# Experts over 512 tokens at once, their sum transposed in one bank and turned back, the combine weight applied last, and a new order of work

## The chip, the cores and the metric

The kernel runs on one core of a Trainium2 chip. The metric is the device time of one execution in microseconds (us). The engines of a core are named as in the profile: PE (TensorE matmul) and PEld (its weight load), DVE (VectorE), ACT (ScalarE), POOL (GpSimd) and SP (SyncE, whose queue issues most DMAs here). They run side by side, each takes its own instructions in program order, and semaphores tie them together.

## The reference

One transformer layer on x of shape (2, 1024, 128), all in float32: a causal attention with 16 heads of 8 dimensions, then a mixture of experts.

```python
x = x + attention(layernorm(x))          # 16 heads, q and k normed, rope, causal
xf = layernorm(x).reshape(-1, 128)       # 2048 tokens
scores = softmax(xf @ gate_w.T)          # 16 experts in 4 groups; the 2 best groups, then the 2 best experts
combine = (one_hot(idx, 16) * weights[..., None]).sum(1)      # (token, expert), two entries not zero
h1 = einsum('td,edi->tei', xf, We1) + be1                     # every expert on every token, i = 64
h3 = einsum('td,edi->tei', xf, We3) + be3
yo = einsum('tei,eid->ted', silu(h1) * h3, We2) + be2
y = einsum('te,ted->td', combine, yo)
z = silu(xf @ ws1 + bs1) * (xf @ ws3 + bs3) @ ws2 + bs2       # shared expert
x = x + (y + z)
```

## The kernel before

The 2048 tokens are four chunks x = 0 to 3 of 512 tokens (four tiles of 128). Each chunk is prepared (norm, q/k/v, rope), goes through attention in four head groups (a = 4x to 4x+3), and then through an epilogue (onT, proj, norm2, x2T, gate, routing, cT) and the experts. In attention, `max` matmuls feed row maxima to DVE (L1157), `scores` matmuls (L783) feed exponentials on ACT (L911), and `pv` matmuls (L801) sum in bank 7; `leave` (L978, o_raw) copies that bank out at the end of a group. So the last row on L978 is the end of attention.

PSUM has eight banks of 512 float32 columns. Bank 7 holds attention's sum, bank 6 the experts' sum y, and the others are shared out.

The 16 experts are eight pairs, so that a pair's inner width is 128; with the shared expert there are UNITS = 9 units. Before the change a unit is worked on for half a chunk (HALF = 256 tokens), which makes 18 steps for each chunk and 72 in all. A step goes like this:

- PE: two matmuls of 256 columns, w1 and w3 against x2T, both into one bank (L838, L839). The trace shows a float32 matmul as two records.
- ACT: mu = (u + b1)/2 (L948), mv = v + b3 (L950), both out of that bank, which is then free; mh = tanh(mu) (L958).
- POOL (chunk 3: DVE): mv = mv * combine weight (L601). The weights have come from DRAM, spread over the partitions (comb_b, four DMAs of 512 KB for a chunk, L681), where the routing's result was stored (L673).
- DVE: mh = (mh + 1) * mu (L1246).
- POOL: mh = mh * mv (L1076).
- PE: two matmuls of 128 columns with mh as the weights and w2 as what moves, added into y, tokens on the partitions (L850). At one step of a chunk the bias be2 is added with four small matmuls (L855).

At the end of a chunk DVE adds bank 6 to xs (L1309, `final`) and SP stores it. mu, mv and mh have MOE_RING = 4 places.

The router's result goes: gate matmuls (L819), gate_read (L1207, L1208), route1 to route3 on DVE (L1218 to L1241, some 35 small operations), cT on PE (L827), combT on ACT (L1010), store and load by DMA, then the first weighting.

The order of work on each engine is the output of `plan()`: a list scheduler over named stages, each with an assumed length (LENGTHS), an urgency out of tables of numbers (PREP_WINDOWS, MOE_WINDOWS and so on) and the stages that it follows. The five engines' programs are that one list, filtered.

## Time and profile before

| | |
|---|---|
| three runs | 459.22, 461.11 (median), 461.4 us |
| the profiled execution | 462.71 us, of which the span on the core is 461.0 us |
| PE busy | 387.2 us (84%) |
| DVE busy | 352.2 us (76%) |
| ACT busy | 273.4 us (59%) |
| POOL busy | 186.8 us (41%) |

The span runs from the first to the last instruction; the remaining 1.7 us lie around it. Busy shares are means over stages in which different engines are the limit, so the stretches below matter more than these. PEclk is the share of full speed that was granted to TensorE; it has two levels, 1.2 and 2.4 GHz, which the rows show as 0.5 and 1.0 or a mix.

### The profile page before, as it was taken

The numbers are of one execution on the slowest core, as the hardware profiler recorded it, in microseconds if no ns is written. First come the engines' busy times: TensorE is split into PE (matmuls) and PEld (weight loads), VectorE is DVE, ScalarE is ACT, GpSimd is POOL, SyncE is SP. The second block draws the span as 40 slices with busy tenths as digits, with TensorE's granted clock in tenths as the row PEclk, the third lists the DMA queues.
The fourth block names the chain that finished last, engine by engine and source line by source line (L and its number), as shares of the span: only waits on it lengthen the run. The fifth ranks groups of instructions, "written<-read, shape, count | busy, mean of one in ns | idle before, by whom it ended". The sixth has DMA issues, their size and how long they took to land.

```text
span 461.0 us, 7965 instructions
## 1 busy us (share of the span) xinstructions
PE 387.2 (84%) x2663; PEld 194.1 (42%) x2663; DVE 352.2 (76%) x757; ACT 273.4 (59%) x483; POOL 186.8 (41%) x277
## 2 busy tenths in 40 slices
PE   3642867679797999999999798889999999986995
PEld 2321322213323443664334334544333273775884
DVE  4778989889878788794387799987875883678396
ACT  2523044621786584757955664439688789864784
POOL 1303926732065225464523130546202244575564
PEclk9765698575889699999999699999999999999998
DMA  5955022000050007000005005300000000800530
GB/s 144 193 101 137 2 60 79 3 1 0 1 138 1 3 19 169 1 1 1 4 23 139 2 1 126 63 1 1 2 2 0 1 3 4 197 11 1 143 67 23
DMA packets 30265, 21.54 MB, mean 47 GB/s; under 512 B 8945, under 2 KB 30098, under 8 KB 30162
## 3 DMA queue, kind: packets, MB, share of 16 engines
q1 hardware_dynamic: 28834, 19.99, 18.6%
q10 hardware_dynamic: 1392, 1.05, 0.9%
q8 instruction: 22, 0.36, 0.4%
q14 instruction: 17, 0.14, 0.1%
HBM read 13.43 MB, written 1.18 MB: 32 GB/s over the span
## 4 chain that ended last, share of the span: by engine, by line
PE 55%; DVE 25%; ACT 8%; issue 7%; POOL 2%; SPq 1%; DMA 1%; POOLq 0%; ACTq 0%; DVEq 0%
PE psum L801 13%; PE psum L783 7%; PE psum L759 7%; PE psum L850 6%; DVE mx_diag L1157 6%; PE psum L838 6%; PE psum L839 5%; DVE mx_full L1157 3%; PE psum L753 3%; PE psum L724 3%; ACT probs L911 2%; DVE nr L1095 2%; DVE mv L601 2%; DVE nr L1096 2%; PE psum L733 1%
## 5 line engine op out<-in xcount | busy, mean ns | idle before, releaser
L911 ACT ACTIVATE probs<-psum 128x1024 f32<-128x1024 f32 x144 | 141.6, 1027 | 58.7 <-PE psum L783 55.4
L1157 DVE TENSOR_REDUCE mx_diag<-psum 128x4 f32<-128x512 f32 (+2 forms) x96 | 96.6, 1039 | 26.4 <-PE psum L759 25.8
L1065 POOL TENSOR_SCALAR_AFFINE_SELECT probs<-probs 128x256 f32<-128x256 f32 (+1 forms) x112 | 47.7, 442 | 108.3 <-ACT probs L911 107.8
L1157 DVE TENSOR_REDUCE mx_full<-psum 128x2 f32<-128x1024 f32 x64 | 75.8, 1218 | 17.0 <-PE psum L759 16.7
L1076 POOL TENSOR_TENSOR mh<-mh,mv 128x256 f32<-128x256 f32 x72 | 55.5, 777 | 77.9 <-DVE mh L1246 69.5
L801 PE MATMUL psum<-probs,v_ones 128*9 128x512 f32 (+3 forms) x768 | 82.1, 519 | 1.5 <-POOL probs L1065 0.8
L783 PE MATMUL psum<-q_st,k_st 64*128 64x512 bf16 (+3 forms) x384 | 59.8, 363 | 9.7 <-ACT probs L911 6.7
L759 PE MATMUL psum<-k_st,q_st 62*128 62x512 bf16 (+3 forms) x384 | 62.7, 357 | 4.4 <-DVE mx_full L1157 2.3
L1246 DVE SCALAR_TENSOR_TENSOR mh<-mh,mu 128x256 f32<-128x256 f32 x72 | 36.5, 523 | 27.0 <-ACT mh L958 26.7
L948 ACT ACTIVATE mu<-psum,b1h 128x256 f32<-128x256 f32 x72 | 33.8, 470 | 37.0 <-PE psum L839 25.0
L850 PE MATMUL psum<-w,mh 128*128 128x128 f32 x288 | 48.1, 295 | 5.6 <-POOL mh L1076 5.5
L838 PE MATMUL psum<-x2T,w 128*128 128x256 f32 x144 | 47.7, 414 | 1.6 <-ACT mv L950 1.6
L601 POOL TENSOR_TENSOR mv<-mv,comb_b 128x256 f32<-128x256 f32 x48 | 35.4, 740 | 27.7 <-ACT mv L950 23.9
L850 PEld LDWEIGHTS psum<-w,mh 128*128 128x128 f32 x288 | 39.3, 194 | 17.3 <-POOL mh L1076 9.5
L839 PE MATMUL psum<-x2T,w 128*128 128x256 f32 x144 | 43.8, 387 | 0.0
L783 PEld LDWEIGHTS psum<-q_st,k_st 64*128 64x128 bf16 x384 | 17.5, 97 | 59.9 <-ACT probs L911 38.8
L753 PE MATMUL psum<-causal_bf,ident_bf 128*128 128x128 bf16 (+1 forms) x192 | 33.1, 259 | 10.3 <-DVE mx_diag L1157 7.1
L950 ACT ACTIVATE mv<-psum,b 128x256 f32<-128x256 f32 x72 | 33.8, 469 | 0.0
L958 ACT ACTIVATE mh<-mu 128x256 f32<-128x256 f32 x72 | 29.7, 418 | 6.8 <-PE psum L855 2.8
L759 PEld LDWEIGHTS psum<-k_st,q_st 62*128 62x128 bf16 x384 | 16.4, 95 | 35.1 <-issue 16.1
L839 PEld LDWEIGHTS psum<-x2T,w 128*128 128x128 f32 x144 | 28.2, 196 | 4.2
L753 PEld LDWEIGHTS psum<-causal_bf,ident_bf 128*128 128x128 bf16 x192 | 13.4, 101 | 39.1 <-DVE mx_diag L1157 18.6
(142 smaller groups left out, 422.4 us busy)
## 6 DMA issues: line engine op xcount, KB each, us to landing
comb_b<-combine_scratch SPq DMA_DIRECT2D x16, 512.0 KB, 8.7
q_st<-parts SPq DMA_DIRECT2D x24, 128.0 KB, 2.5
k_st<-parts SPq DMA_DIRECT2D x18, 128.0 KB, 2.4
w<-in_We SPq DMA_DIRECT2D x3, 512.0 KB
k_st<-in_c_pad SPq DMA_DIRECT2D x2, 512.0 KB, 8.0
out<-xs SPq DMA_DIRECT2D x4, 256.0 KB, 4.5
xs<-in_x SPq DMA_DIRECT2D x3, 256.0 KB, 10.3
k_st<-parts ACTq DMA_DIRECT2D x6, 128.0 KB, 3.5
```

Source lines behind the costliest of these rows:

```text
L601: engine.tensor_tensor(mv[:, at % MOE_RING, :], mv[:, at % MOE_RING, :], comb_b[:, half, u, :], ALU.mult).then_inc(weighted, 1)
L753: pe.matmul(v, ident_bf[:, :], causal_bf[:, :].unsqueeze(1).broadcast_to([P, nm, P]), start=True, stop=False, skip_group_check=True)
L759: last = pe.matmul(w[:, par, i * keys:(i + 1) * keys], q_st[r, x % 2, 2 * g + m, q0:q0 + P], k_st[r, b, 2 * g + m, k0:k0 + keys], start=(w ...
L783: last = pe.matmul(w[:, par, col:col + cols], k_st[rows(par), b, 2 * g + m, kt * P:(kt + 1) * P], q_st[rows(par), x % 2, 2 * g + m, q0:q0 ...
L801: last = pe.matmul(acc[32 * j:32 * j + VC, q0:q0 + cols], v_ones[:, b, kt, G * g + j, :], probs[:, n % P_RING, j % 2, col:col + cols], sta ...
L838: pe.matmul(w[:, 0:HALF], w1[:, u, :], rhs, start=True, stop=True)
L839: pe.matmul(w[:, HALF:CH], w3[:, u, :], rhs, start=True, stop=True).then_inc(work_full, 1)
L850: last = pe.matmul(y[:, tok * P:(tok + 1) * P], mh[:, at % MOE_RING, t * P:(t + 1) * P], w2[:, u, :], start=(n == 0 and t == 0), stop=(n = ...
L911: act.activation(probs[:, n % P_RING, :, :], wpair("scores", (s, i)), ACT.Exp, scale=SCALE).then_inc(exp_done, 1)
L1065: last = pool.affine_select(out=v, in_=v, compare_op=ALU.is_ge, fill=0.0, base=0, pattern=[[0, v.shape[1]], [1, P]], channel_multiplier=-1)
L1076: pool.tensor_tensor(mh[:, at % MOE_RING, :], mh[:, at % MOE_RING, :], mv[:, at % MOE_RING, :], ALU.mult).then_inc(h_ready, 1)
L1157: dve.tensor_reduce(dst[:, qt, :, pairs[0]:pairs[0] + nm], w, AX.X, ALU.max).then_inc(max_free, 1)
```

## The change

A unit is now worked on for the whole chunk of 512 tokens, 9 steps for a chunk and 36 in all.

- PE: v = w3 against x2T, 512 columns, into a bank of its own (`moeV`), and u = w1 against x2T into another (`moeU`).
- ACT: mv = (v + b3)/2 out of the first (`moe_v`), which frees it; mh = tanh((u + b1)/2) straight out of the second (`moe_t`), and, after a wait for that, mh = mh + 1. mu is gone.
- DVE: mv = (u + b1) * mv, with u still in PSUM (`moe_a`). This frees the second bank.
- POOL: mh = mh * mv (`moe_g`), and then the combine weight, mh = mh * comb_b (`moe_h`; in chunk 3 on DVE, `moe_h_dve`). The weight comes last, so everything ahead of it can run without it. mh has nine places now (T_RING), mv four (V_RING).
- PE: one matmul of 512 columns with w2 as the weights and mh as what moves, so y is transposed in bank 6 (features on the partitions). The bias is one matmul of 512 columns.
- At a chunk's end ACT copies bank 6 to yT (`y_leave`), PE turns it back in four transposes (`yturn`), and DVE adds it to xs.
- The weights come in two DMAs of 1 MB for a chunk (before: four of 512 KB).
- The shared unit is the first of a chunk (n = 0) and takes no weight.
- The assumed lengths and all urgency tables have new numbers, so the order is new everywhere, in attention too. rden has two places.

```diff
-P_RING, MOE_RING = 6, 4
+P_RING, V_RING, T_RING = 6, 4, 9
...
 def unit(n):
 
-    return (n, PAIRS) if n < 2 else divmod(n - 2, PAIRS)
-
+    return (n - 1) % UNITS
...
-MOE_WINDOWS = ((57.8, 72.7), (115.5, 150.2), (242.3, 392.7), (261.5, 603.0))
...
+MOE_WINDOWS = ((119.1, 212.3), (178.6, 259.5), (211.2, 383.4), (419.9, 419.9))
...
-            add("moe", (x, n), key, ("x2T_read", x), back("moe", 1))
-            pair = unit(n)[1] < PAIRS
-            add("moe_u", (x, n), key, ("halved", 0), ("moe", (x, n)), back("moe_h", MOE_RING), back("moe_u", 1))
-            add("moe_t", (x, n), key, ("moe_u", (x, n)), back("moe_y", MOE_RING), back("moe_t", 1))
...
+            add("moeV", (x, n), key, ("x2T_read", x), back("moeU", 1))
+            add("moe_v", (x, n), key, ("halved", 0), ("moeV", (x, n)), back("moe_g", V_RING), back("moe_t", 1))
+            add("moeU", (x, n), key, ("moeV", (x, n)))
+            add("moe_t", (x, n), key, ("moeU", (x, n)), ("moe_v", (x, n)), back("moe_y", T_RING))
+            add("moe_a", (x, n), key, ("moe_t", (x, n)), back("moe_a", 1))
+            add("moe_g", (x, n), key, ("moe_a", (x, n)), back("moe_g", 1))
...
-            engine.wait_ge(act_u, at + 1)
-            engine.tensor_tensor(mv[:, at % MOE_RING, :], mv[:, at % MOE_RING, :], comb_b[:, half, u, :],
-                                 ALU.mult).then_inc(weighted, 1)
+            u = unit(n)
+            if n == 1:
+                engine.wait_ge(ld_combine, 32 * (x + 1))
+            engine.wait_ge(gate_done, UNITS * x + n + 1)
+            h = mh[:, (UNITS * x + n) % T_RING, :]
+            engine.tensor_tensor(h, h, comb_b[:, u, :], ALU.mult).then_inc(weighted, 1)
...
+                        src = combine_dram[x].rearrange("(m e) q -> e m q", e=2)[e]
+                        sp.dma_start(comb_b[64 * e:64 * e + 64, :, :], src.partition_broadcast(64)
+                                     ).then_inc(ld_combine, 16)
...
-                rhs = x2T[:, x % 2, half * HALF:(half + 1) * HALF]
-                pe.matmul(w[:, 0:HALF], w1[:, u, :], rhs, start=True, stop=True)
-                pe.matmul(w[:, HALF:CH], w3[:, u, :], rhs, start=True, stop=True).then_inc(work_full, 1)
+                pe.matmul(w, (w1 if kind == "moeU" else w3)[:, unit(n), :], x2T[:, x % 2, :], start=True, stop=True
+                          ).then_inc(work_full, 1)
...
-                pe.wait_ge(h_ready, at + 1)
-                for t in range(2):
-                    tok = 2 * half + t
-                    last = pe.matmul(y[:, tok * P:(tok + 1) * P], mh[:, at % MOE_RING, t * P:(t + 1) * P], w2[:, u, :],
-                                     start=(n == 0 and t == 0), stop=(n == 2 * UNITS - 1), skip_group_check=True)
+                    pe.wait_ge(gate_done, at + 1)
+                else:
+                    pe.wait_ge(weighted, PAIRS * x + n)
+                last = pe.matmul(y, w2[:, unit(n), :], mh[:, at % T_RING, :], start=(n == 0), stop=(n == UNITS - 1),
+                                 skip_group_check=True)
                 if n == BIAS_STEP:
                     pe.wait_ge(work_read_act, frees("act", turned("cT", x)))
-                    for t in range(TPC):
-                        last = pe.matmul(y[:, t * P:(t + 1) * P], combT[:, t * P:(t + 1) * P], b2[:, :],
-                                         start=False, stop=False, skip_group_check=True)
+                    last = pe.matmul(y, b2[:, :], combT[:, :], start=False, stop=False, skip_group_check=True)
...
-                act.activation(mu[:, at % MOE_RING, :], wbank("moe", (x, n))[:, 0:HALF], ACT.Identity,
-                               bias=b1h[:, u:u + 1], scale=0.5)
-                act.activation(mv[:, at % MOE_RING, :], wbank("moe", (x, n))[:, HALF:CH], ACT.Identity,
-                               bias=b3[:, u:u + 1]).then_inc(act_u, 1)
+                if at >= V_RING:
+                    act.wait_ge(gate_done, at - V_RING + 1)
+                act.activation(mv[:, at % V_RING, :], wbank("moeV", (x, n)), ACT.Identity,
+                               bias=b3h[:, unit(n):unit(n) + 1], scale=0.5).then_inc(work_read_act, 1)
...
-                act.activation(mh[:, at % MOE_RING, :], mu[:, at % MOE_RING, :], ACT.Tanh).then_inc(act_t, 1)
...
+                act.activation(t, wbank("moeU", (x, n)), ACT.Tanh, bias=b1h[:, unit(n):unit(n) + 1], scale=0.5
+                               ).then_inc(act_t, 1)
+                act.wait_ge(act_t, 2 * at + 1)
+                act.activation(t, t, ACT.Identity, bias=ones_col[:, 0:1]).then_inc(act_t, 1)
...
+                    act.copy(yT[:, :], bank(Y_BANK)).then_inc(y_left, 1)
...
+                    pool.wait_ge(u_read, at + 1)
+                    t = mh[:, at % T_RING, :]
+                    pool.tensor_tensor(t, t, mv[:, at % V_RING, :], ALU.mult).then_inc(gate_done, 1)
...
-                dve.wait_ge(act_t, at + 1)
-                dve.scalar_tensor_tensor(out=mh[:, at % MOE_RING, :], in0=mh[:, at % MOE_RING, :], scalar=1.0,
-                                         in1=mu[:, at % MOE_RING, :], op0=ALU.add, op1=ALU.mult).then_inc(gated, 1)
...
+                dve.wait_ge(act_t, 2 * at + 2)
+                v = mv[:, at % V_RING, :]
+                dve.scalar_tensor_tensor(out=v, in0=wbank("moeU", (x, n)), scalar=b1[:, unit(n):unit(n) + 1], in1=v,
+                                         op0=ALU.add, op1=ALU.mult).then_inc(u_read, 1)
...
-                    dve.wait_ge(y_done, 2 * UNITS * (arg + 1))
-                    dve.tensor_tensor(xs[:, arg, :, :], bank(Y_BANK).rearrange("p (t d) -> p t d", t=TPC),
-                                      xs[:, arg, :, :], ALU.add).then_inc(out_ready, 1)
+                    dve.wait_ge(work_full, turned("yturn", arg))
+                    dve.tensor_tensor(xs[:, arg, :, :], wbank("yturn", arg).rearrange("p (t d) -> p t d", t=TPC),
+                                      xs[:, arg, :, :], ALU.add).then_inc(work_read_dve, 1)
```

What the new numbers do to the order is seen in the engines' rows. First PE, at the end of the program, the last expert steps of chunk 3 (before: L838 and L839 make u and v, L850 adds to y).

```order
L850 MATMUL psum<-w,mh 128x128 x4
L838 MATMUL psum<-x2T,w 128x256
L839 MATMUL psum<-x2T,w 128x256
L850 MATMUL psum<-w,mh 128x128 x2
L838 MATMUL psum<-x2T,w 128x256
L839 MATMUL psum<-x2T,w 128x256
L850 MATMUL psum<-w,mh 128x128 x8
```

The same place now, from chunk 3's cT (L828) on; L837 makes v or u, L848 adds to y, L852 is the bias and L725 the transposes.

```order
L828 MATMUL psum<-ident,lg 16x128 x4
L837 MATMUL psum<-x2T,w 128x512 x3
L848 MATMUL psum<-mh,w 128x512
L837 MATMUL psum<-x2T,w 128x512
L725 MATMUL psum<-ident,yT 128x128 x4
L837 MATMUL psum<-x2T,w 128x512 x8
L848 MATMUL psum<-mh,w 128x512 x2
L852 MATMUL psum<-combT,b 128x512
L848 MATMUL psum<-mh,w 128x512 x7
L725 MATMUL psum<-ident,yT 128x128 x4
```

All additions to chunk 3's y have moved behind all of its u and v, and a turning back stands at the very end.

Second, DVE at the end of the program. Before, each (mh + 1) * mu (L1246) is followed by a weighting (L601):

```order
L1246 SCALAR_TENSOR_TENSOR mh<-mh,mu 128x256
L601 TENSOR_TENSOR mv<-mv,comb_b 128x256 x2
L1246 SCALAR_TENSOR_TENSOR mh<-mh,mu 128x256
L601 TENSOR_TENSOR mv<-mv,comb_b 128x256
L1246 SCALAR_TENSOR_TENSOR mh<-mh,mu 128x256
L1309 TENSOR_TENSOR xs<-psum,xs 128x512
```

Now, from the last row of chunk 3's routing (L1246 of the changed kernel) on; L1252 is `moe_a`, L603 the weighting and L1317 the add to xs.

```order
L1246 TENSOR_TENSOR lg<-lg 128x64
L1252 SCALAR_TENSOR_TENSOR mv<-psum,b,mv 128x512 x5
L1317 TENSOR_TENSOR xs<-psum,xs 128x512
L1252 SCALAR_TENSOR_TENSOR mv<-psum,b,mv 128x512 x4
L603 TENSOR_TENSOR mh<-mh,comb_b 128x512 x2
L1252 SCALAR_TENSOR_TENSOR mv<-psum,b,mv 128x512
L603 TENSOR_TENSOR mh<-mh,comb_b 128x512 x6
L1317 TENSOR_TENSOR xs<-psum,xs 128x512
```

The weightings have moved behind nearly all other expert work of the chunk, and the first `moe_a` behind the routing frees a bank that cT is to be written to.

Third, DVE early on, between the third and the fourth attention group of chunk 0 (rden marks a group). Before:

```order
L1184 RECIPROCAL rden<-psum 128x16
L1186 TENSOR_TENSOR o_norm<-psum,rden 128x4x32
L1157 TENSOR_REDUCE mx_full<-psum 128x2 x5
L1128 TENSOR_REDUCE ssum<-sq 128x128
L1157 TENSOR_REDUCE mx_full<-psum 128x2
L1132 TENSOR_SCALAR hvar<-ssum 128x128
...
L1157 TENSOR_REDUCE mx_diag<-psum 128x4 x2
```

Now:

```order
L1189 RECIPROCAL rden<-psum 128x16
L1191 TENSOR_TENSOR o_norm<-psum,rden 128x4x32
L1161 TENSOR_REDUCE mx_full<-psum 128x2
L1110 BN_STATS stats<-xs 128x6 x4
...
L1161 TENSOR_REDUCE mx_full<-psum 128x2 x2
```

Chunk 3's head sums and their reciprocal roots (L1128 and L1132 on, 12 operations) have moved behind chunk 0's attention; its norm (L1110 on) has come into this place.

## Rows read from the trace of the kernel before

**Rows 1.** Four stretches: length, PE, PEld, DVE, ACT, POOL busy, clock, DMA, GB/s.

```profile
0.00:159.40 159.40, 110.83 (x653) 44.31 (x654) 129.86 (x295) 67.17 (x122) 63.27 (x79) 0.74 0.27 62
159.40:394.40 235.00, 220.10 (x1687) 101.70 (x1686) 175.78 (x347) 162.37 (x251) 84.33 (x147) 0.97 0.12 29
394.40:424.00 29.60, 24.19 (x144) 20.14 (x142) 22.97 (x76) 18.19 (x47) 17.20 (x24) 1.00 0.29 68
424.00:461.00 37.00, 32.05 (x186) 27.96 (x185) 23.55 (x41) 25.63 (x67) 21.99 (x29) 0.92 0.31 73
```

**Rows 2.** Timeline from attention's end on: start, us, instruction.

```profile
394.43 0.57 ACT L978 COPY o_raw<-psum 128x512 f32<-128x512 f32 x1
...
421.98 0.23 DVE L1241 TENSOR_TENSOR lg<-lg 128x64 f32<-128x64 f32 x1
...
425.39 1.06 PE L827 MATMUL psum<-ident,lg 128*16 128x128 f32 x4
...
428.66 4.19 SPq L681 DMA_DIRECT2D comb_b<-combine_scratch  x4
...
437.38 0.75 DVE L601 TENSOR_TENSOR mv<-mv,comb_b 128x256 f32<-128x256 f32 x2
...
457.63 0.69 DVE L1309 TENSOR_TENSOR xs<-psum,xs 128x512 f32<-128x512 f32 x1 [1.61 <-PE psum L850]
```

**Rows 3.** Timeline of PE while it has no gaps.

```profile
182.10 0.71 PE L850 MATMUL psum<-w,mh 128*128 128x128 f32 x4
182.74 1.15 PE L855 MATMUL psum<-b,combT 17*128 17x128 f32 x8
183.82 0.66 PE L724 MATMUL psum<-ident,o_raw 128*128 128x128 f32 x4
...
186.98 0.59 PE L838 MATMUL psum<-x2T,w 128*128 128x256 f32 x2
187.41 0.59 PE L839 MATMUL psum<-x2T,w 128*128 128x256 f32 x2
...
188.26 0.70 PE L838 MATMUL psum<-x2T,w 128*128 128x256 f32 x2
...
189.32 0.39 PE L783 MATMUL psum<-q_st,k_st 64*128 64x512 bf16 x2
```

**Rows 4.** Groups of instructions by line and shape: busy us, mean ns | idle before.

```profile
L911 ACT ACTIVATE probs<-psum 128x1024 f32<-128x1024 f32 x144 | 141.6, 1027 | 58.7 <-PE psum L783 55.4 <-PE psum L801 2.5
L1157 DVE TENSOR_REDUCE mx_full<-psum 128x2 f32<-128x1024 f32 x64 | 75.8, 1218 | 17.0 <-PE psum L759 16.7
L1076 POOL TENSOR_TENSOR mh<-mh,mv 128x256 f32<-128x256 f32 x72 | 55.5, 777 | 77.9 <-DVE mh L1246 69.5 <-DVE mv L601 6.8
L1246 DVE SCALAR_TENSOR_TENSOR mh<-mh,mu 128x256 f32<-128x256 f32 x72 | 36.5, 523 | 27.0 <-ACT mh L958 26.7
L948 ACT ACTIVATE mu<-psum,b1h 128x256 f32<-128x256 f32 x72 | 33.8, 470 | 37.0 <-PE psum L839 25.0 <-POOL mh L1076 11.5
L978 ACT COPY o_raw<-psum 128x512 f32<-128x512 f32 x16 | 9.4, 586 | 15.6 <-PE psum L801 15.5
L588 POOL TENSOR_TENSOR roped<-qk,g_sin 128x512 f32<-128x512 f32 x6 | 6.3, 1068 | 0.0
L1142 DVE TENSOR_TENSOR resid<-psum,parts 128x512 f32<-128x512 f32 x8 | 5.5, 683 | 2.8 <-ACT parts L939 2.8
L1047 POOL TENSOR_TENSOR xs<-xs,bo_b 128x512 f32<-128x512 f32 x4 | 5.1, 1269 | 22.1 <-ACT xn L970 13.3 <-DMA bo_b<-in_bo 8.8
```

**Rows 5.** comb_b from 424 us on: duration ns min/median/max, and its DMAs' landing.

```profile
L601 DVE TENSOR_TENSOR mv<-mv,comb_b x16: 411/944/949, 437.4 to 454.7; 128x256 f32<-128x256 f32 x16
...
DMA to landing us min/median/max: 5.8/7.8/9.5
```

**Rows 6.** Timeline of PE behind its longest gap of the last stage.

```profile
423.51 0.71 PE L850 MATMUL psum<-w,mh 128*128 128x128 f32 x4 [3.53 <-POOL mh L1076]
...
427.10 0.92 PE L838 MATMUL psum<-x2T,w 128*128 128x256 f32 x2
```

186 lines of the change are left out of this document (91 added, 95 removed).

## Prediction, made before the changed kernel ran

> **What bounds the kernel now.** I read the busy time of stretches first, cut where attention changes its limit. Up to 159.4 us DVE is busy 129.9 us and PE 110.8 us at a mean clock of 0.74; from there to the last attention group PE is busy 220.1 of 235.0 us at 0.97 [rows 1]. So the middle is PE's, with 14.9 us of gaps, and the start is mostly DVE's. Then I read the timeline from 394.43 us, where attention's sum leaves for the last time, to the end: 66.6 us in which only experts and chunk 3's epilogue run [rows 2]. PE is busy 56.2 of them (24.19 + 32.05) [rows 1]. A chain runs through this stage. The last routing row ends at 422.2, cT starts at 425.39, the loads of the combine weights are issued from 428.66 on, the first weighting starts at 437.38, the last add at 457.63, and the end is 3.4 us behind that [rows 2]. Between 437 and 457 the steps follow each other at about 1.2 us, DVE's 0.41 plus a weighting whose median is 0.94 [rows 5], and PE needs 0.86 + 0.43 for the same step, so both are full there. Last I read the costs of single kinds of instruction.
>
> **PE's work.** A 256-column float32 matmul takes 0.43 us between two of its kind (186.98 to 187.41), and a u/v pair that stands between other matmuls takes 1.06 (188.26 to 189.32), 0.20 above 2 x 0.43. A y step takes 0.64 (182.10 to 182.74), the old bias 1.08, four transposes 0.6 to 0.66 [rows 3]. A 512-column matmul isn't in the trace; I take 4 x 0.215 = 0.86 us back to back, and 0.96 between others; the bounds are 0.86 and 1.06. Then a unit costs 2 x 1.06 + 2 x 0.64 = 3.40 us before and 3 x 0.96 = 2.88 now, 18.7 less over 36 units. Four biases give 0.5, four turnings back take 2.5. PE loses about 17 us of work, or 7 us if a 512-column matmul costs 1.06.
>
> Where that falls matters. Counting in the engines' order, before the last `leave` there were 39 u/v pairs and 35 y steps; now there are 45 single u or v matmuls and 19 y matmuls. That is 41.3 + 22.4 + 2.2 = 65.9 us before and 43.2 + 18.2 + 1.9 + 1.2 (two turnings) = 64.5 now. The saving has been spent on doing three more units' u and v ahead of the last stage, which is where it pays.
>
> **The other engines.** ACT: 0.47 for each 256-column read with a bias; 512 columns cost 0.586 as a copy, and 1024 cost 1.027, so 512 more columns cost 0.44 and a 512-column one with a bias about 0.68 [rows 4]. Three of them and one wait for its own result make 2.0 to 2.2 us a unit, against six of at most 0.47 = 2.8. DVE: 2 x 0.523 becomes one of 0.683, the nearest row with a PSUM and an SBUF input of 512 columns [rows 4]; the weighting in chunk 3 becomes 8 of 0.41 + 0.27 = 0.68 in place of 16 of 0.41 to 0.95 [rows 5]. POOL: 2 x 0.777 becomes one of 1.07 to 1.27 [rows 4]; I take 1.15. All three lose work, and none of that is a term unless it stands in the chain below.
>
> **Up to the last `leave` (394.4 us).** PE's work is 1.4 us less. Chunk 0's fourth attention group now has some 8 us less DVE work ahead of it: 12 operations of the head roots, the head sums and three reductions of 1.22 [rows 4] have moved behind, a norm has come in. That work must still be done, and so must the qkv of chunk 3 that moved with it, in the next 50 us, where DVE and PE are both near full [rows 1]. The bounds for this part: 10 us gained, if two thirds of the middle's 14.9 us of gaps go; 8 us lost, if the new order leaves as many gaps again for half of it. I take 3 gained.
>
> **The last stage, as a chain from `leave`.** (a) To the last routing row: 27.8 us before (394.43 to 422.2). POOL's products are now 1.15 instead of 0.78 [rows 4], and small DVE operations wait for them; +1.0, so 28.8. (b) To cT: before 3.2 us, as cT stood behind a y step that waited for POOL. Now cT needs a bank that the first `moe_a` behind the routing frees: 0.7 + 0.1, so 29.6. (c) cT to the issue of the loads: 3.3 (425.39 to 428.66), 32.9. (d) Issue to the first weighting: the first half came within 8.7 (to 437.38) and the last of the four DMAs by 432.2 + 9.5 = 441.7, 13.0 behind the first issue [rows 2, 5]. Now DVE waits for both halves, in two DMAs with larger pieces. Bounds 8.7 and 13.0; I take 10.5: 43.4. (e) The first weighting 0.7, then eight y matmuls and the bias, 9 x 0.86 = 7.7: 51.8. DVE's 0.68 stays ahead of PE's 0.86. (f) `y_leave` 0.2 + 0.6, turning back 0.1 + 0.7, the add's wait 0.1, and 3.4 from the add to the end: 56.9.
>
> The cover: what PE has to do before (e) is 26 u/v matmuls and 9 y matmuls and a bias at about 0.9, four transposed blocks 2.5, proj, gate and cT 2.8 = 37.7 us, and during the routing it runs dry: the four banks open to the experts then hold u's that only DVE can release, and DVE is routing. From the gate on PE has 11 matmuls, 9.5 us, for a routing of 12 to 13 us. With that gap of 3 to 4 us and a slow stretch behind it PE is ready at 42 to 43.6 us, level with (d). I add 1 us for the two being level: 57.9, against 66.6. **The last stage gains 8.7 us.**
>
> **Sum.** 461.0 - 3 - 8.7 = 449.3 us of span; with 1.7 around it 451.0, against the profiled execution's own 462.7. That execution lies 1.6 us above the median of the three runs, so the median of the changed kernel should be **449.4 us**.
>
> **Rivals.**
> - *The gaps in the middle go too.* DVE, ACT and POOL all have less to do and the combine weights no longer hold up a step. For it: POOL's products waited 69.5 us for DVE and ACT's reads 11.5 for POOL [rows 4]. Against it: most such waits cost PE nothing. With 10 us gained there: 449.4 - 7 = 442 us.
> - *POOL's wider products hold DVE up.* The DVE weighting of 256 columns takes 0.41 alone and has a median of 0.944 beside POOL [rows 5]: it waits for what POOL is doing. If the small DVE operations of chunk 3's norm and routing wait for a product of 1.15 to 1.27 us as that one waited for 0.78, eight such meetings cost about 0.4 us more each, 3 to 4 us on (a) where I have 1.0. For it: POOL has some eight products left in that time. Against it: the weightings themselves meet little POOL work now, as the last `moe_g` are nearly done by then. 449.4 + 2.6 = 452 us. SBUF — State Buffer in the Trainium skill (Who interferes with whom) says as much: DVE with two SBUF inputs and GpSimd lock each other out for a whole instruction, however long it is.
> - *The clock takes the gain.* A gap of 3.53 us on PE before 423.51 was followed by matmuls at half speed: the pair at 427.10 lasted 0.92 instead of 0.59, at 1.2 GHz, and the last stretch had a mean of 0.92 [rows 6, 1]. Now PE has such a gap in the routing and perhaps another before the loads land, and all of (e) stands behind it with no cover. The 7.7 us of (e) at half speed for a good part, and nothing gained in the middle: 449.4 + 3 + 5 = 457 us. TensorE: Matmul & The Clock Gate in the Trainium skill (HAM oscillation — how this bites in real kernels) has the same mechanism, waits that throttle the clock again and leave the next matmuls slow; by that rule, too, (e) would start slow after a wait for the loads.
> - *Slower: u's bank waits for DVE.* ACT used to free a unit's one bank. Now a unit takes two, and u's is held through tanh, the added one and DVE's queue, in which row maxima of 1.22 us stand [rows 4]. Experts share these banks with maxima and scores. If each of the 18 units beside the maxima in chunks 0 and 1 costs PE a whole such reduction, that is 22 us; with the last stage's gain it comes to 449.4 + 3 + 22 = 474, and 468 if it is 0.9 us each. From (8.7 / 18 =) 0.5 us a unit on, the kernel is slower than before. Against it: DVE is busy 176 of 235 us there, and PE has other groups' scores and maxima to go on with.
>
> **How the numbers follow.** The forecast has 0.40, and its own range is 445 to 454. POOL's products have 0.12 (452). The gaps going has 0.17 (442, down to 439), the clock 0.19 (457), the bank 0.10 (468 to 474); 0.02 is left. A difference under 0.5%, 2.3 us, is about what a measurement of this kernel can't tell from none, so faster means under 458.8. Of the clock's 0.19 I count 0.12 as faster and 0.07 as the same, and 0.01 to 0.02 of the rest as the same: faster 0.81, same 0.09, slower 0.10. The range of 8 in 10 reaches from 440 to 459.
>
> **What would show it.** In the profile after: PE's busy time near 370 us; u, v and y matmuls as two records at 0.43 us spacing; the last o_raw copy at 388 to 395 us; some 57 to 58 us from there to the end; from cT to the first weighting 13 to 14 us; nine y matmuls in a row at 0.43 us a record and with hardly a gap; `moe_a` near 0.68 and POOL's products at 1.07 to 1.27. Wrong would be: DVE waits for tanh growing while PE's waits for `moe_a` come up by tens of us (the bank), the granted clock under 0.9 in the last 15 us (the clock), or an o_raw copy that is later than 400 us, where my reading of the order before attention's end fails.

## The result, and the profile of the changed kernel

The changed kernel takes 459.87 us (median of 20 executions, 454.97 to 461.91), the kernel before 461.42 us (20 executions, 459.05 to 464.27). The ratio of the mean times is 0.9945, with a 95% interval of 0.9918 to 0.9972: about half a per cent faster (a third of one by the medians). The ratios here and below leave out executions in a slow state, at a lower clock, and one of these (520.6 us, with only chunk 3 split) is left out of its range too. The forecast was 449.4 us. The profiled execution took 455.45 us (span 453.7), 4.4 us less than the median, whereas that of before lay 1.3 us above its own.

First the busy time of four stretches, cut at the last `leave` and ahead of cT as in [rows 1] (length, then PE, PEld, DVE, ACT and POOL busy, clock, DMA share, GB/s):

```profile
0.00:159.40 159.40, 113.98 (x686) 44.27 (x686) 132.14 (x323) 78.20 (x138) 56.72 (x76) 0.82 0.34 73
159.40:391.40 232.00, 213.43 (x1481) 70.89 (x1480) 168.36 (x307) 151.51 (x190) 87.24 (x119) 0.96 0.11 25
391.40:421.00 29.60, 25.91 (x73) 11.08 (x74) 19.26 (x64) 17.55 (x30) 14.67 (x12) 0.94 0.25 49
421.00:453.70 32.70, 25.19 (x60) 9.96 (x58) 15.06 (x23) 14.74 (x23) 14.18 (x11) 0.95 0.40 82
```

The last `leave` has moved from 394.4 to 391.4 us. The middle has 18.6 us of gaps on PE (14.9 before), the last stretch 7.5 (5.0 before). The clock column tells that TensorE ran at its half level, 1.2 GHz, for a part of each of the last three stretches.

The timeline of PE shows the largest of these gaps, in chunks 1, 2 and 3 (start, us, instruction; in brackets the wait ahead of it and what ended it):

```profile
285.37 1.12 PE L848 MATMUL psum<-mh,w 128*128 128x512 f32 x2 [2.04 <-POOL mh L603]
...
289.44 2.08 PE L848 MATMUL psum<-mh,w 128*128 128x512 f32 x2
...
401.48 1.13 PE L848 MATMUL psum<-mh,w 128*128 128x512 f32 x2 [2.52 <-POOL mh L603]
402.53 1.41 PE L852 MATMUL psum<-combT,b 17*128 17x512 f32 x2
403.87 4.20 PE L848 MATMUL psum<-mh,w 128*128 128x512 f32 x6
407.92 0.60 PE L725 MATMUL psum<-ident,w_raw 128*128 128x128 f32 x4
...
422.44 0.61 PE L828 MATMUL psum<-ident,lg 128*16 128x128 f32 x4 [0.69 <-DVE mv L1252]
...
438.87 1.12 PE L848 MATMUL psum<-mh,w 128*128 128x512 f32 x2 [2.63 <-DVE mh L603]
439.93 1.26 PE L852 MATMUL psum<-combT,b 17*128 17x512 f32 x2
441.12 7.79 PE L848 MATMUL psum<-mh,w 128*128 128x512 f32 x14
```

A 512-column matmul is two records here. All three gaps end with the first product with a combine weight, L603, and behind each the clock is at its half level for a while: at 289.44 one y matmul takes 2.08 instead of 1.13 us, at 403.87 three take 4.20, and at 441.12 seven take 7.79 where 0.9 each would be 6.3. The granted clock is 0.68 from 285.4 to 296 us, 0.74 from 401.5 to 408 and 0.85 from 438.9 to 450, and still 1.00 up to the end of each gap. Worked out from these, the half level lasted 6.8, 3.4 and 3.3 us and cost half of that, 6.8 us in all; the three waits come to 7.2. Each time the product itself had waited for the load (POOL at 284.06 for 2.29 us and at 400.16 for 4.17, DVE at 438.13 for 2.01). At the second place this also reaches DVE, which is at chunk 3's norm; first POOL's timeline, then DVE's:

```profile
400.16 4.93 POOL L603 TENSOR_TENSOR mh<-mh,comb_b 128x512 f32<-128x512 f32 x4 [4.17 <-DMA comb_b<-combine_scratch]
```

```profile
400.06 0.16 DVE L1099 SCALAR_TENSOR_TENSOR nr<-seed 128x4 f32<-128x4 f32 x1
400.26 1.18 DVE L1100 TENSOR_TENSOR nr<-nr,rstd 128x4 f32<-128x4 f32 x1
401.48 1.19 DVE L1101 SCALAR_TENSOR_TENSOR rstd<-nr,seed 128x4 f32<-128x4 f32 x1
402.70 1.19 DVE L1127 SCALAR_TENSOR_TENSOR shift<-mean_var,rstd 128x4 f32<-128x4 f32 x1
...
421.49 0.23 DVE L1246 TENSOR_TENSOR lg<-lg 128x64 f32<-128x64 f32 x1
```

Three operations of 0.16 us take 1.2 beside POOL's four products.

The groups of the changed kernel that answer to [rows 4] (busy us, mean ns, idle time ahead and its releasers):

```profile
L837 PE MATMUL psum<-x2T,w 128*128 128x512 f32 x144 | 75.3, 628 | 2.8 <-ACT mv L947 2.2 <-DVE mv L1252 0.2
L848 PE MATMUL psum<-mh,w 128*128 128x512 f32 x72 | 42.0, 693 | 7.2 <-POOL mh L603 4.6 <-DVE mh L603 2.6
L956 ACT ACTIVATE mh<-psum,b1h 128x512 f32<-128x512 f32 x36 | 24.7, 687 | 34.4 <-PE psum L837 34.3
L947 ACT ACTIVATE mv<-psum,b3h 128x512 f32<-128x512 f32 x36 | 24.4, 679 | 10.4 <-PE psum L837 10.1
L959 ACT ACTIVATE mh<-mh,ones_col 128x512 f32<-128x512 f32 x36 | 26.0, 722 | 1.2
L1252 DVE SCALAR_TENSOR_TENSOR mv<-psum,b,mv 128x512 f32<-128x512 f32 x36 | 26.4, 745 | 21.6 <-ACT mh L959 21.3
```

### The profile page after: what moved, and what is told of

Read it like the earlier page. It is cut to its first block, busy times and chain, and to the rows that moved or that the text cites. A ratio compares the mean times of both kernels' runs of the same rounds, so it can differ in the third digit from the quotient of the medians.

```text
span 453.7 us, 6878 instructions
## 1 busy us (share of the span) xinstructions
PE 378.5 (83%) x2295; PEld 136.2 (30%) x2295; DVE 334.8 (74%) x715; ACT 262.0 (58%) x379; POOL 172.8 (38%) x217
## 4 chain that ended last, share of the span: by engine, by line
PE 43%; DVE 24%; ACT 11%; DMA 10%; issue 6%; POOL 4%; SPq 2%; ACTq 0%; DVEq 0%
PE psum L802 10%; DMA comb_b<-combine_scratch 8%; PE psum L784 7%; DVE mx_full L1161 7%; PE psum L848 6%; ACT probs L910 6%; PE psum L837 5%; PE psum L760 5%; DVE mx_diag L1161 5%; PE psum L754 3%; PE psum L725 3%; ACT mh L956 1%; DVE nr L1099 1%; DMA xs<-in_x 1%; DVE nr L1100 1%
## 5 line engine op out<-in xcount | busy, mean ns | idle before, releaser
L837 PE MATMUL psum<-x2T,w 128*128 128x512 f32 x144 | 75.3, 628 | 2.8 <-ACT mv L947 2.2
L1081 POOL TENSOR_TENSOR mh<-mh,mv 128x512 f32<-128x512 f32 x36 | 45.9, 1280 | 74.7 <-DVE mv L1252 74.5
L848 PE MATMUL psum<-mh,w 128*128 128x512 f32 x72 | 42.0, 693 | 7.2 <-POOL mh L603 4.6
L956 ACT ACTIVATE mh<-psum,b1h 128x512 f32<-128x512 f32 x36 | 24.7, 687 | 34.4 <-PE psum L837 34.3
L1252 DVE SCALAR_TENSOR_TENSOR mv<-psum,b,mv 128x512 f32<-128x512 f32 x36 | 26.4, 745 | 21.6 <-ACT mh L959 21.3
L784 PEld LDWEIGHTS psum<-q_st,k_st 64*128 64x128 bf16 x384 | 16.5, 94 | 70.6 <-ACT probs L910 52.5
L603 POOL TENSOR_TENSOR mh<-mh,comb_b 128x512 f32<-128x512 f32 x24 | 30.1, 1269 | 7.5 <-DMA comb_b<-combine_scratch 6.5
L837 PEld LDWEIGHTS psum<-x2T,w 128*128 128x128 f32 x144 | 23.6, 191 | 29.1 <-issue 12.0
L947 ACT ACTIVATE mv<-psum,b3h 128x512 f32<-128x512 f32 x36 | 24.4, 679 | 10.4 <-PE psum L837 10.1
L959 ACT ACTIVATE mh<-mh,ones_col 128x512 f32<-128x512 f32 x36 | 26.0, 722 | 1.2
L802 PEld LDWEIGHTS psum<-probs,v_ones 128*9 128x9 f32 x768 | 13.7, 89 | 30.0 <-issue 28.4
L926 ACT COPY qk<-psum 128x256 f32<-128x256 f32 x16 | 6.0, 378 | 28.4 <-POOL roped L594 13.4
## 6 DMA issues: line engine op xcount, KB each, us to landing
xs<-in_x SPq DMA_DIRECT2D x3, 256.0 KB, 10.4
```

The lines of the kernel that those rows point to most:

```text
L603: engine.tensor_tensor(h, h, comb_b[:, u, :], ALU.mult).then_inc(weighted, 1)
L784: last = pe.matmul(w[:, par, col:col + cols], k_st[rows(par), b, 2 * g + m, kt * P:(kt + 1) * P], q_st[rows(par), x % 2, 2 * g + m, q0:q0 ...
L802: last = pe.matmul(acc[32 * j:32 * j + VC, q0:q0 + cols], v_ones[:, b, kt, G * g + j, :], probs[:, n % P_RING, j % 2, col:col + cols], sta ...
L837: pe.matmul(w, (w1 if kind == "moeU" else w3)[:, unit(n), :], x2T[:, x % 2, :], start=True, stop=True).then_inc(work_full, 1)
L848: last = pe.matmul(y, w2[:, unit(n), :], mh[:, at % T_RING, :], start=(n == 0), stop=(n == UNITS - 1), skip_group_check=True)
L956: act.activation(t, wbank("moeU", (x, n)), ACT.Tanh, bias=b1h[:, unit(n):unit(n) + 1], scale=0.5).then_inc(act_t, 1)
```

## The experiments

Every kernel was timed in five rounds beside the kernel before, whose median was 461.2 to 462.1 us. Behind the unchanged kernel, the first seven of the table change the loads or the waits, the others the shapes, the ring and the order. The kernel before has four DMAs on two semaphores for a chunk, by halves of the tokens; "split loads" gives the changed kernel four again, by units. Two kernels here leave a part of the result wrong and serve as probes alone: "no load for chunk 3" and "split, old y form".

| kernel | median (range), us | ratio to before, 95% |
|---|---|---|
| changed kernel again | 458.19 (452.22 to 461.22) | 0.9877 (0.9820 to 0.9934) |
| **split loads** | **444.83 (444.12 to 445.61)** | **0.9634 (0.9602 to 0.9667)** |
| split, but all awaited | 457.35 (451.71 to 460.12) | 0.9863 (0.9803 to 0.9922) |
| only chunk 3 split | 452.33 (450.72 to 454.46) | 0.9788 (0.9742 to 0.9834) |
| no load for chunk 3 | 455.89 (451.75 to 456.78) | 0.9852 (0.9809 to 0.9895) |
| loads in quarters | 443.63 (442.54 to 447.62) | 0.9640 (0.9595 to 0.9685) |
| PE kept busy, unsplit | 449.61 (448.16 to 454.68) | 0.9759 (0.9702 to 0.9816) |
| before, all awaited | 486.46 (481.08 to 488.50) | 1.0534 (1.0486 to 1.0583) |
| split, u/v 256 wide | 444.70 (441.80 to 447.10) | 0.9646 (0.9599 to 0.9693) |
| split, old y form | 444.27 (441.93 to 447.38) | 0.9647 (0.9596 to 0.9698) |
| split, ACT 256 wide | 454.76 (453.00 to 456.96) | 0.9859 (0.9828 to 0.9890) |
| split, DVE and POOL 256 wide | 447.30 (446.21 to 449.59) | 0.9699 (0.9670 to 0.9727) |
| split, all 256 wide | 456.59 (455.79 to 457.62) | 0.9899 (0.9871 to 0.9927) |
| split, ring of 5 | 448.56 (447.98 to 450.31) | 0.9728 (0.9700 to 0.9757) |
| old tables, unsplit | 480.31 (478.58 to 481.87) | 1.0394 (1.0352 to 1.0436) |
| old tables, split | 469.87 (466.23 to 470.34) | 1.0142 (1.0104 to 1.0180) |

### The same kernel again

No edit.

> The changed kernel itself, profiled a second time. Its first profiled execution took 455.45 us and its 20 timed ones have a median of 459.9 (454.97 to 461.91). Theory 1, the spread is the granted clock over the same order of work: the time from start to the last o_raw copy and the time from there to the end both move with the clock of their stretch, by up to 7 us in all, and this profile reads 455 to 462. Theory 2, the spread is a real second course (a DMA that lands later and with it a different wait): the clocks are alike within 0.01 and one wait is longer by some us. Ratio to before 0.991 to 0.998 by either.

The second profile has a span of 456.1 us at the same mean clock, 0.910. Its o_raw copies run from 77.8 to 394.0 us, against 76.1 to 391.4: of the 2.4 us between the two, 1.7 are there at the first copy, and behind the last one the two are alike (62.1 and 62.3). No single wait is longer, so the second theory has nothing for it, but the first isn't shown either, as neither profile caught one of the executions at 459 to 461. The three gaps and the slow stretches behind them are in both.

### Loads in two parts

```diff
-            if n == 1:
-                engine.wait_ge(ld_combine, 32 * (x + 1))
+            if n in (1, 5):
+                engine.wait_ge(ld_combine[n // 5], 32 * (x + 1))
...
-                    for e in range(2):
-                        src = combine_dram[x].rearrange("(m e) q -> e m q", e=2)[e]
+                    for half in range(2):
+                        for e in range(2):
+                            src = combine_dram[x].rearrange("(m e) q -> e m q", e=2)[e][4 * half:4 * half + 4, :]
```

> The combine weights of a chunk come in four DMAs (units 0 to 3 of both halves of the partitions, then units 4 to 7) on two semaphores, so that the first weighting waits for half as much. Theory 1, the landing is on the path: PE waited 2.63 us for the first weighting in the profile of the changed kernel, so the first weighting comes 2 to 5 us earlier and the kernel gains 1.5 to 2.6 us (ratio to the kernel before 0.989 to 0.992). Theory 2, the last stage is paced by ACT's 1.91 us for each unit and by POOL's products up to 437: nothing is gained, the wait of 2.63 us turns up between the y steps (0.9945 as without the edit).

444.8 us: 13.4 less than the changed kernel in the same rounds (11.2 by the ratios of means), five times the most that either theory gave. I had looked at the last stage alone. The timeline of PE at the three places of above (one source line lower by number) says where it is:

```profile
283.78 1.13 PE L849 MATMUL psum<-mh,w 128*128 128x512 f32 x2
284.83 1.12 PE L853 MATMUL psum<-combT,b 17*128 17x512 f32 x2
...
288.24 2.84 PE L849 MATMUL psum<-mh,w 128*128 128x512 f32 x6
...
400.07 0.66 PE L726 MATMUL psum<-ident,w_raw 128*128 128x128 f32 x4 [1.00 <-ACT w_raw L972]
...
414.75 0.61 PE L829 MATMUL psum<-ident,lg 128*16 128x128 f32 x4 [0.66 <-DVE mv L1253]
...
420.47 7.24 PE L838 MATMUL psum<-x2T,w 128*128 128x512 f32 x16
427.55 1.02 PE L849 MATMUL psum<-mh,w 128*128 128x512 f32 x2
429.09 1.12 PE L849 MATMUL psum<-mh,w 128*128 128x512 f32 x2 [0.53 <-DVE mh L603]
```

The waits of 2.04 and 2.52 us are gone, that of 2.63 is 0.53, and no y matmul is at half clock. From the eleventh to the twelfth o_raw copy, where chunk 1's y steps stand, it takes 40.2 us instead of 46.4, and from the last copy to the end 56.3 instead of 62.3. In the second, chunk 2's weightings start at 391.39 and not at 400.16, so they are nearly done when DVE comes to the norm, and x2T is turned 13.2 us behind the last copy instead of 16.5. In the third, it takes 28.4 us from cT to the end instead of 31.3. That is 6.2, 3.3 and 2.9 us for waits of 2.04, 2.52 and 2.63. With the waits the spread has gone: 1.5 us over six executions, against 7 to 9 for the changed kernel.

The Trainium skill has both sides of this (Perfetto Trace Analysis, DMA Optimizations): larger DMAs use the memory's bandwidth better, and splitting DMAs into smaller chunks may allow some of them to start sooner. This edit does two things, it splits the DMAs and it lets the first weighting wait for half of them; the next run tells the two apart.

### Four DMAs, all awaited

```diff
+            if n == 1:
+                engine.wait_ge(ld_combine[0], 32 * (x + 1))
+                engine.wait_ge(ld_combine[1], 32 * (x + 1))
```

> Four DMAs of 512 KB for each chunk as in the kernel with split loads, but the first weighting waits for all four. Theory 1, the split pays because less is waited for: the gain is gone, 456 to 460 us as the changed kernel. Theory 2, four smaller DMAs land sooner than two large ones: 445 to 450.

457.35 us, within the noise of the changed kernel's 458.2. The gaps are back (2.38, 2.12 and 2.47 us at the same three places), each with half clock behind it. It is what is waited for, not the size of a DMA: splitting alone gained nothing here.

This profile shows something more. Its waits in chunks 2 and 3 are a little shorter than those of the changed kernel's profile, but from the last copy to the end it takes 65.1 us and not 62.3: the three y matmuls behind the bias in chunk 2 take 5.49 us instead of 4.20, and in chunk 3 it is 11.7 us from the first weighted y matmul to the end of the last, instead of 10.0. So after a wait of the same length the half level can last longer or shorter. That would spread a kernel's times with the order of work and the waits unchanged; for the changed kernel's executions of 459 to 461 us it isn't shown.

### The kernel before, all awaited

```diff
-                engine.wait_ge(ld_combine[half], 32 * (x + 1))
+                engine.wait_ge(ld_combine[0], 32 * (x + 1))
+                engine.wait_ge(ld_combine[1], 32 * (x + 1))
```

> The kernel before, whose weighting of the first half of the tokens waits for the loads of both halves too; nothing else is changed. Theory 1, waiting for the whole chunk is what the changed kernel lost, whatever the shapes of its instructions: 4 to 12 us slower than before, 466 to 473. Theory 2, it costs only where the new order has put PE close behind the landing: within 1.5 us of before, 460.5 to 463.5.

486.5 us: 24.6 slower than before, twice what the first theory gave. The old kernel, in which the weight comes ahead of the gate and the rings have four places, can bear this wait even less: PE has five waits of 2.4 to 4.3 us for L1077's products (3.45 us at 184.93, 4.30 at 413.73). That fits the view that putting the weight last bought slack, which the coarse load spent, but the two kernels differ in their rings and their order as well, and no run changes the place of the weight alone.

### Only chunk 3 split; no load for chunk 3

```diff
+                    for half, (lo, hi) in enumerate(((0, 8),) if x < 3 else ((0, 4), (4, 8))):
```

> Only chunk 3's combine weights come in four DMAs with two semaphores; those of chunks 0 to 2 as in the changed kernel. With all chunks split the kernel took 444.8 us against 458 to 460. Theory 1, three waits of PE for the first weighting make the difference (2.04 us at 285.4, 2.52 at 401.5, 2.63 at 438.9 in the changed kernel's profile, each followed by a stretch at half clock): the last one alone gives 2.6 + 1.7 = 4.3 us, so 454 to 456. Theory 2, the last stage alone decides: 445 to 449. Theory 3, nothing for the last one alone, as with no load at all for chunk 3 (455.9): 456 to 459.

452.33 us, 5.9 less than the changed kernel run again, in other rounds, and a little more than the 4.3 expected. There is no profile to tell its places by.

```diff
-                engine.wait_ge(ld_combine, 32 * (x + 1))
+                engine.wait_ge(ld_combine, 32 * min(x + 1, 3))
...
+                    if x == 3:
+                        continue
```

> Chunk 3's combine weights are not loaded: its weightings read those of chunk 2, which are in place, so the output of chunk 3 isn't the reference's. It is the ceiling of what the route from routing over cT to the landed loads costs. Theory 1, the landing alone holds PE up: 2.6 us gained against the changed kernel and no more, as POOL's last products end at 437. Theory 2, the y steps can then slip in among the u and v steps, which ACT paces at 1.91 us a unit and which leave PE idle: 7 to 9 us gained, most of the 9.7 us that the y steps took behind the last u.

455.89 us, 2.3 less: the first theory by its size, though the intervals of this kernel and of the changed one overlap. Why a load that isn't there helps so little, DVE's timeline of this kernel shows:

```profile
437.24 0.75 DVE L1254 SCALAR_TENSOR_TENSOR mv<-psum,b,mv 128x512 f32<-128x512 f32 x1 [1.16 <-ACT mh L961]
439.14 0.75 DVE L1254 SCALAR_TENSOR_TENSOR mv<-psum,b,mv 128x512 f32<-128x512 f32 x1 [1.15 <-ACT mh L961]
439.81 2.36 DVE L603 TENSOR_TENSOR mh<-mh,comb_b 128x512 f32<-128x512 f32 x2
```

In DVE's order the first weighting stands behind the last gated sum of the chunk, and these come every 1.91 us, when ACT has done its three operations. From the copy of cT it is 12.9 us to it, with split loads too (415.48 to 428.36), and 15.0 in the changed kernel. So the load holds chunk 3 up by 2.1 us, and then ACT is the limit.

These two runs don't agree on chunk 3's share: 5.9 us with its loads split and 2.3 with no load at all. The traces put it at 3.0. From cT to the end it is 28.3 us with no load, 28.4 with all loads split and 31.3 in the changed kernel, so the split takes all that there is to take in chunk 3. In the profile of the kernel without the load, 1.3 us of this went again in chunk 2, where the half level lasted longer (three y matmuls in 5.49 us, not 4.20). The rest of the difference is within the spread of these kernels, 4 to 5 us.

### Quarters

```diff
+            if n % 2:
+                engine.wait_ge(ld_combine[n // 2], 32 * (x + 1))
...
+                    for part in range(4):
```

> The combine weights of a chunk in eight DMAs of 256 KB on four semaphores, two units at a time. Base: the kernel with four DMAs and two semaphores, 444.8 us. Theory 1, what is waited for still costs: the first weighting comes another 1 to 3 us sooner behind cT (12.9 us in chunk 3 of the base), 442 to 444. Theory 2, SP's four more issues of 0.62 us and PE's cover (no wait of PE for a weighting over 0.6 us is left in the base) take it back: 444 to 446.

443.63 us: the same as two parts within the intervals, though it lies in the first theory's range. In chunk 3 the first weighting starts 12.8 us behind the start of the copy of cT (418.42 to 431.17), as with two parts (12.9). No wait for a load was left to take.

### PE kept busy in two of the waits

```diff
+            def keep_busy(count):
+                for _ in range(count):
+                    pe.matmul(psum[:, 0, :], ident_bf[:, :], k_st[:, 0, 0, 0:CH], start=True, stop=True)
...
+                if (kind, arg) in (("moe_y", (2, 1)), ("moe_y", (3, 1))):
+                    keep_busy(12)
```

> The changed kernel with 12 bfloat16 matmuls of 512 columns (0.21 us each, 2.6 us) into a free bank ahead of the y steps for which PE waited 2.52 and 2.63 us in chunks 2 and 3. The wait stays, but PE has work in it. Theory 1, the half clock behind those waits is due to them: no half clock at 403 to 407 and 441 to 444, 2.5 to 3.5 us gained, median 455 to 457. Theory 2, the slow stretches come whatever PE did before: nothing gained, 458 to 460.

449.61 us. The loads are as late as before, but the y matmuls run at full clock (timeline of PE):

```profile
431.68 2.54 PE L857 MATMUL psum<-k_st,ident_bf 128*128 128x512 bf16 x11
434.12 1.12 PE L848 MATMUL psum<-mh,w 128*128 128x512 f32 x2
435.18 1.12 PE L852 MATMUL psum<-combT,b 17*128 17x512 f32 x2
436.23 6.28 PE L848 MATMUL psum<-mh,w 128*128 128x512 f32 x14
```

Seven y matmuls take 6.28 us instead of 7.79. From the last copy to the end it is 58.9 us against 62.3: 3.4, as the first theory had it, and the half clock behind these two waits is shown to be due to them. The median gained 8.6 us though, and lies below the 455 to 457 of that theory. 3.2 more are in chunk 1, where nothing was added: there PE's gap was 1.24 us in this profile, and no half clock followed. The rest isn't settled; the executions of 459 to 461 us of the changed kernel, whose mean clocks are lower (0.89 to 0.91), weren't caught in a profile.

### Narrow matmuls; the old form of y

All further runs with new shapes start from the kernel with split loads, whose times spread least.

```diff
+                for cols in (slice(0, CH // 2), slice(CH // 2, CH)):
+                    last = pe.matmul(w[:, cols], (w1 if kind == "moeU" else w3)[:, unit(n), :], x2T[:, x % 2, cols],
+                                     start=True, stop=True)
```

> The kernel with split loads (444.8 us), with each u or v of 512 columns written as two matmuls of 256 columns with the same weights. Theory 1, one matmul of 512 columns saves 0.1 to 0.2 us against two of 256: 72 of them, PE busy 7 to 14 us more, 449 to 455. Theory 2, a 512-column float32 matmul is carried out as two passes anyway and only the change from one kind of matmul to the next costs: the same within 1.5 us, 443.5 to 446.

```diff
-                last = pe.matmul(y, w2[:, unit(n), :], mh[:, at % T_RING, :], start=(n == 0), stop=(n == UNITS - 1),
-                                 skip_group_check=True)
+                for t in range(TPC):
+                    last = pe.matmul(y[:, t * P:(t + 1) * P], mh[:, at % T_RING, t * P:(t + 1) * P], w2[:, unit(n), :],
+                                     start=(n == 0 and t == 0), stop=(n == UNITS - 1), skip_group_check=True)
```

> The kernel with split loads (444.8 us), with the y step as four matmuls of 128 columns with the tokens as weights, the form of before (and the bias likewise); the turning back is left in, so the output's blocks of 128 x 128 are transposed. Theory 1, the y form is what the restructuring saves on PE: 1.28 to 1.4 us a unit instead of 1.06 between others and 0.95 in a row, 8 to 14 us more PE work, of which 7 to 12 shows: 452 to 457. Theory 2, PE has gaps to take it up outside the last nine steps: 446 to 449.

444.70 and 444.27 us: both edits cost nothing, as the second theory had it for u and v; for the old y it is less than either theory gave. The timelines of PE, first with narrow u and v, then with the old y:

```profile
291.52 1.13 PE L840 MATMUL psum<-x2T,w 128*128 128x256 f32 x4
292.59 0.39 PE L761 MATMUL psum<-k_st,q_st 62*128 62x512 bf16 x2
```

```profile
286.36 1.16 PE L850 MATMUL psum<-w,mh 128*128 128x128 f32 x8
287.45 0.39 PE L761 MATMUL psum<-k_st,q_st 62*128 62x512 bf16 x2
```

From its start to the next kind of matmul, 512 columns of float32 take 1.07 us in two instructions and 1.09 in four; in one it is 1.06 (286.86 to 287.92 with split loads). What PE does with a unit hasn't become cheaper by the wider instructions, except that a y step in one piece has fewer neighbours of another kind than one in two.

### The other engines narrow

On ACT (v, tanh and the added one, all three alike):

```diff
+                for cols in (slice(0, CH // 2), slice(CH // 2, CH)):
+                    last = act.activation(t[:, cols], wbank("moeU", (x, n))[:, cols], ACT.Tanh,
+                                          bias=b1h[:, unit(n):unit(n) + 1], scale=0.5)
```

> Base: the kernel with split loads, 444.8 us. ACT's three operations of a unit (v, tanh, the added one) as two of 256 columns each, so about 2.8 us instead of 2.07 for a unit, 25 us more of ACT over 36 units. Theory 1, ACT paces the last stage (1.91 us a unit with eight units in a row, while PE could do one in 1.8): 6 us more there, and 1 to 4 before: 451 to 455. Theory 2, ACT has room (59% busy) and waits absorb it: 444 to 447.

On DVE and POOL (the gated sum, POOL's product and the weighting):

```diff
+            for cols in (slice(0, CH // 2), slice(CH // 2, CH)):
+                last = engine.tensor_tensor(h[:, cols], h[:, cols], comb_b[:, u, cols], ALU.mult)
```

> Base: the kernel with split loads, 444.8 us. DVE's gated sum and POOL's and DVE's products as two instructions of 256 columns each (0.523 for 0.74 on DVE, 0.777 for 1.27 on POOL in the profiles): 10 us more of DVE, some 17 of POOL. Theory 1, the narrower POOL products let DVE in sooner and cost nothing: 443 to 446. Theory 2, DVE is the bound up to 159 us and POOL's moe_g and weighting stand between chunk 2's units: 448 to 452.

Both, and PE's u and v:

> Base: the kernel with split loads, 444.8 us. Both edits above and u and v on TensorE as two matmuls of 256 columns: every instruction of the experts is half as wide, in the new order and with the weight last. Theory 1, width is what the restructuring gains: 455 to 462, the kernel before. Theory 2, the order and the place of the weight gain it, and width only what ACT shows alone: 449 to 455.

ACT alone costs 9.9 us, DVE and POOL 2.5 (between the two theories), and all together, with PE's u and v, 11.8, in the first theory's range. Even so this last kernel is 4.9 us faster than the one before in the same rounds. That much is left for the order, the place of the weight and all else that is new, which aren't told apart. Each ACT operation is now 0.46 to 0.50 us twice, instead of 0.68 to 0.72 once (groups with ACT 256 wide):

```profile
L965 ACT ACTIVATE mh<-mh,ones_col 128x256 f32<-128x256 f32 x72 | 32.7, 500 | 1.2
L960 ACT ACTIVATE mh<-psum,b1h 128x256 f32<-128x256 f32 x72 | 30.2, 474 | 27.0 <-PE psum L838 26.9
L949 ACT ACTIVATE mv<-psum,b3h 128x256 f32<-128x256 f32 x72 | 29.7, 462 | 6.9 <-PE psum L838 6.9
```

That is 92.6 us for 75.1, 17.5 more, of which 10 show in the time. ACT was busy 59% of the span, and I had entered its saving as no term of the sum. The wide form gained its time on ACT. But the sum of the first theory is right and its places are not: from the first o_raw copy to the last it is 315.8 us with ACT narrow and 309.8 with split loads, so 6.0 of it lie there, where ACT has attention's exponentials beside the experts, and from the last copy to the end 59.7 against 56.3, so 3.4 lie in the last stage.

### A ring of five

```diff
-P_RING, V_RING, T_RING = 6, 4, 9
+P_RING, V_RING, T_RING = 6, 4, 5
```

> Base: the kernel with split loads, 444.8 us. The ring of products mh has 5 places instead of 9. Up to chunk 3 the order is the same but for two places; in chunk 3, three of the last units' u and v come only behind y steps, and so behind the landing of the combine weights. Theory 1, the ring is what keeps PE and ACT in work while the weights come: 3 to 5 us slower, 448 to 450. Theory 2, the last y steps are short enough that it costs ACT's time of one unit or nothing: 444 to 446.5.

3.7 us slower, as the first theory had it. ACT's read waits for a y step, so PE stands still for 2.17 us ahead of the last units' u and v (428.66), and in the end PE waits 0.4 to 0.8 us for each weighting.

### The old tables

```diff
-PREP_WINDOWS = ((-395.5, -202.0), (-206.6, -128.2), (59.9, 126.4), (336.9, 345.6))
+PREP_WINDOWS = ((-341.8, -177.2), (-238.2, -151.9), (-24.9, 47.7), (282.6, 300.0))
...
-PV_LAG = 133.7
+PV_LAG = 49.3
```

> The restructured experts with the tables of the kernel before (the four windows and the lag of pv): what the restructuring does without the new order. Theory 1, the gain is in the restructuring and the order only spends it: time 457 to 462, within 0.5% of the changed kernel. Theory 2, the new order is what pays: 464 to 475, slower than both, as the old windows set experts beside maxima and leave the last stage long. Theory 3, the new order costs something that the restructuring has to pay for: below 456.

> The tables of the kernel before (windows, lag of pv) in the restructured kernel, with split loads: the pair to the old tables with the loads in one piece (480.3 us) as the kernel with split loads (444.8) is to the changed kernel (459). Theory 1, the loads cost the old tables as much as they cost the kernel before when it had to wait for all (24 us): 456 to 464. Theory 2, the order costs its 20 us whatever the loads do, and the split gives 10 to 14 as it does in the new order: 466 to 471.

480.3 us with the loads in one piece, 469.9 with them split. The split gives 10.4, as in the new order (13.4), and the order costs 22 to 25 us with either: the second theory both times, the first time beyond its range. In the restructured kernel the old numbers are a bad order. (The assumed lengths stayed the new ones.) How the old structure would run in the new order wasn't tried, so how much of these 22 to 25 us is the order's own merit, and how much only that numbers have to fit their structure, stays open.

## Why the prediction was wrong

**Up to the last `leave`: the number right, by luck.** 3 us were forecast and 3.0 measured. As the prediction says, the early gain of the order had to be paid back: the fifth o_raw copy came at 145.7 us instead of 159.4, the sixth at 182.7 instead of 182.2. But from the first copy to the last it took 318.2 us before, 315.3 in the changed kernel and 309.8 with split loads. So 3 is the balance of two things that are not in the sum: some 8 us gained, of which 6.0 go again when ACT's operations are narrow, and 5.5 lost at chunk 1's wait for the loads.

**The cost of a matmul: mis-sized, at its bound.** I took 0.96 us for 512 columns between others, with bounds of 0.86 and 1.06. Between attention's scores, maxima and pv it is mostly 1.06, with one such neighbour 0.96, and 0.86 in a row; the prediction's own pair of u and v, 0.20 above 2 x 0.43, had said 1.06. PE's busy time fell by 8.7 us (387.2 to 378.5), not by 17. That is near the 7 given for the upper bound, but by luck: that bound's own terms give 7.9 + 0.5 - 2.5 = 5.9, and with split loads, where no y matmul behind those waits is at half clock, PE is busy 373.2 us, 14.0 less than before. Cutting the matmuls differently changed no time; what 0.1 us more or less for each of them would do wasn't tried.

**(a) To the last routing row: 28.8 forecast, 30.3 measured.** The term for POOL's products was 1.0. Three of the norm's operations lost a whole product each, 3.1 us, because chunk 2's loads came late and its four weightings ran in a row beside the norm. The y matmuls ahead of x2T's turning were at half clock. The mechanism of the second rival was right, and the late load is what brought it there: with split loads (a) takes 27.2 us, so even the 1.0 wasn't needed.

**(c) and (d): 13.8 from cT to the first weighting forecast, 15.7 measured** (422.44 to 438.13). From issue to weighting it was 12.83, near the bound of 13.0 and not the 10.5 taken. And PE's cover was counted in PE's time; ACT paces it at 1.91 us a unit, so with split loads it is still 13.6 us from cT to the first weighting (414.75 to 428.36).

**(e) and (f): 8.4 and 5.1 forecast, 10.8 and 4.8 measured.** The nine y matmuls are in a row, but from 441 to 444 us at the half level of the clock. This was the third rival, and its size in this one place, 1.5 us over seven matmuls and 0.15 in the bias, is small. The other 0.7 is the cost at full clock: 8.4 us for the nine in the kernel with PE kept busy (434.12 to 442.51), and not 9 x 0.86.

**What failed is the step "the loads", term (d), and its reach.** I priced the wait for both halves once, in chunk 3, at 1.8 us more than the first half needs, and wrote, in favour of a rival, that "the combine weights no longer hold up a step". They hold one up in chunks 1 and 2 as well, two waits that the sum had at nothing, and each time the half clock follows. With split loads all three are gone or short, and the kernel takes 13.4 us less in the same rounds; the profiles show 12.4 of it at the three places, for 7.2 us of waits and an estimated 6.8 lost at half clock, not all of which reaches the end.

**The second error has the other sign.** Without the waits the kernel is at 444.8, 4.6 below the forecast, although PE saved less than I took. Among what I had entered as nothing is ACT's saving, on the ground that ACT was busy 59% of the span: 9.9 us by the run with ACT narrow. These two errors don't close the sum. The forecast with the waits added and ACT's saving taken off would be 449.4 + 13.4 - 9.9 = 452.9, and 459.9 was measured. The 7 us between the two are in part PE's saving, taken at 17 us and 14.0 at full clock, and in part a median above the profiled execution; for the rest no run gives a place.

**The median.** For a profiled execution the forecast was 451.0, and it took 455.45: 4.4 of the miss, all of it behind the last `leave` (62.3 us for 57.9). The other 6 us are that the profiled execution of before lay 1.6 us above the median of its three runs, and this one 4.4 below its own. A profile of before cannot show this. With split loads the spread went too; why a typical execution of the changed kernel is slower than the one profiled stays open.

**The rivals.** The bank of u didn't bind: PE's waits for `moe_a` come to 4.2 us, weight loads included. The gaps of the middle didn't go; the gain ahead of the last `leave` that the first rival asked for was there (some 8 us), and chunk 1's wait hid it. The clock came nearest, 457 against 459.9, by its mechanism in three places and not one.
